# The first two steps of a fused attention and sparse feed-forward kernel rewritten as programs of their own

## The chip, the cores and the metric

The kernel runs on one core of one Trainium2 chip. The metric is the device time of one execution in microseconds (us), the median over the runs.

## The reference

Two branches read the same normalised rows; their sum is added to the input. Cut to what matters:

```python
xn = layernorm(x)                              # x: 4096 rows of 512
# attention branch
q, k, v = xn @ Wq, xn @ Wk, xn @ Wv            # 16 heads of 32; rotary on q and k
# chunks of 128 rows, with a state kv carried from chunk to chunk
out = (q * q_decay) @ kv + ((q @ k.T) * dmask) @ v
kv  = r_C * kv + (k * k_decay).T @ v
attn = rms_norm(out) @ Wo
# sparse feed-forward branch; W_syn 2048x512, W_out 512x2048
ternary(W) = clip(round(W / mean|W|), -1, 1) * mean|W|
z = xn @ ternary(W_syn).T + b_syn
hidden = where(z >= 204th largest of the row, relu(z), 0)
ffn = layernorm(xn + hidden @ ternary(W_out).T + b_out)
result = x + attn + ffn
```

## The kernel before

The 4096 rows are 32 tiles of 128. Every engine runs a program written out by hand: a prologue, then 34 calls of `step`. In step s four tiles are in work: `a` = s+2 (normalised and turned), `b` = s+1 (projections q, k, v and the four z pieces, numbers 0 to 6), `t` = s (attention, search for the threshold), `u` = s-1 (threshold applied, hidden rows split in a high and a low half and turned by DMA, `Wo`), and `d` = s-2 (`network`: the second feed-forward product, 32 matmuls `p_ffn`, and the output). Engines meet by counting semaphores; each engine and each DMA queue works strictly in the order of its program.

The prologue prepares the weights and the first tile up to its z. The mean of |W_syn| gives its threshold (`syn_thr`). ScalarE (ACT) takes row sums of |W|, TensorE adds them across partitions, and VectorE forms the threshold. Then VectorE (`ternary`) and ACT (`sign`, with `ternary_of_signs` on VectorE) make the ternary weights, which are turned by TensorE or by DMA transposes (`synT0`, `synT2`; `outT0` to `outT3`). The four quarters of W_out are prepared during steps 0 and 1, where memory is tight: they pass through places that later hold something else. Quarter 1 (`outT1`) sits in the low half of `hl`, so the first `lo_ready` (tile 0's low half, on GpSimd, which the page calls POOL) waits until that transpose has landed; VectorE's `below` for tile 1 writes `masked` and waits for this `lo_ready`. `hT`, which takes the turned hidden rows, lies over the buffer `area1[:, 3N:4N]`, through which quarters 0 and 1 of W_out are loaded (`out_in[0]`, loaded twice, and `out_in[1]`).

SP issues nearly all DMAs; ACT issues only the four loads of W_syn, among its first sums. `network(0)` starts when all four `outT` and the high half of tile 0 in `hT` are there, and needs the low half for its second 16 matmuls.

```python
wait(dve, "lo_ready", t, 1, 0)       # below(t): tile t-1's low half is made
if u.n == 0:
    pool.wait_ge(S["outT1"], 16)     # tile 0's low half
for q in range(4):
    pe.wait_ge(S[f"outT{q}"], 16)    # network, tile 0
```

## Time and profile before

| | us |
|---|---|
| median of 3 runs | 1045.2 (1045.08 to 1045.99) |
| the profiled execution: its time | 1045.96 |
| the profiled execution: its span | 1044.0 |
| busy TensorE (PE) | 971.1 (93%) |
| busy VectorE (DVE) | 760.7 (73%) |
| busy ScalarE (ACT) | 560.8 (54%) |
| busy GpSimd (POOL) | 694.9 (67%) |

The span is what the profiler covers; some 2 us lie around it. The shares are averages over stages: in 40 slices of the span TensorE is busy 1, 7, 6 and 7 tenths in the first four and 9 or more from the sixth to the 37th.

### The profile page before, as it was taken

What the parts mean: (1) busy time and instruction counts of PE and PEld (TensorE: products, weight loads), DVE (VectorE), ACT (ScalarE), POOL (GpSimd) and SP (SyncE); (2) the same over time, 40 slices, a digit from 0 to 9 for tenths busy, and PEclk for the clock granted to TensorE, in tenths of its full rate; (3) what the DMA queues carried; (4) which work ended last, traced back from release to release, by engine and by line L of the source; (5) the groups of instructions that cost most, each with busy time, mean ns of one, the idle gap of its engine ahead of it and who ended that gap; (6) DMA issues with size and microseconds to landing.
All of it is one profiled execution on the core that took longest, in us unless ns stands there. A gap on an engine that the chain in (4) does not pass through costs nothing.

```text
span 1044.0 us, 18566 instructions
## 1 busy us (share of the span) xinstructions
PE 971.1 (93%) x6608; PEld 493.5 (47%) x6608; DVE 760.7 (73%) x2153; ACT 560.8 (54%) x715; POOL 694.9 (67%) x617
## 2 busy tenths in 40 slices
PE   1767799999999999999999999999999999999875
PEld 0333455554555555554555555554555555554432
DVE  2577767777877777777877777777877777776762
ACT  3877664654454665654455655654455655654421
POOL 1334777777778777777778777777777777777522
PEclk9978899999999999999999999999999999999976
DMA  9785756546455456545654555455554455555322
GB/s 295 258 201 91 145 88 112 101 92 112 100 103 96 83 96 112 97 97 111 97 107 78 96 101 111 92 101 111 93 111 89 81 104 110 89 106 101 72 51 60
DMA packets 328782, 113.65 MB, mean 109 GB/s; under 512 B 314736, under 2 KB 314992, under 8 KB 327792
## 3 DMA queue, kind: packets, MB, share of 16 engines
q1 hardware_dynamic: 326576, 108.25, 53.5%
q10 hardware_dynamic: 2112, 4.19, 1.3%
q8 instruction: 53, 0.87, 0.3%
q14 instruction: 41, 0.34, 0.1%
HBM read 25.38 MB, written 8.39 MB: 32 GB/s over the span
## 4 chain that ended last, share of the span: by engine, by line
PE 84%; DVE 1%; DMA 1%; issue 0%; POOL 0%; ACT 0%; SPq 0%; POOLq 0%; DVEq 0%
PE proj L735 42%; PE p_ffn L828 22%; PE p_wo L864 10%; PE p_av L803 3%; PE sbank L794 3%; PE p_av L849 2%; PE sbank L743 1%; PE sbank L885 1%; DMA area<-hl 1%; DVE area L1136 0%; PE sbank L897 0%; ACT hl L475 0%; PE p_wo L814 0%; POOL c L636 0%; SPq L299 0%
## 5 line engine op out<-in xcount | busy, mean ns | idle before, releaser
L735 PE MATMUL proj<-wqkv,xT 128*128 128x512 f16 x1152 | 257.6, 383 | 0.7 <-DVE wqkv L967 0.4
L735 PE MATMUL proj<-wsynT,xT 128*128 128x512 f16 x1024 | 246.2, 384 | 1.4 <-DVE area L1022 0.9
L828 PE MATMUL p_ffn<-woutT,area 128*128 128x512 f16 x1024 | 235.6, 385 | 10.9 <-DMA area<-hl 10.9
L735 PEld LDWEIGHTS proj<-wqkv,xT 128*128 128x128 f16 x1152 | 113.2, 99 | 131.7 <-issue 4.0
L468 ACT ACTIVATE Pr<-area,c 128x2048 f16<-128x2048 f32 x32 | 64.1, 2003 | 199.0 <-DVE c L1130 193.4
L828 PEld LDWEIGHTS p_ffn<-woutT,area 128*128 128x128 f16 x1024 | 101.9, 104 | 121.6 <-DMA area<-hl 11.1
L735 PEld LDWEIGHTS proj<-wsynT,xT 128*128 128x128 f16 x1024 | 93.2, 99 | 126.1 <-issue 35.0
L1022 DVE SCALAR_TENSOR_TENSOR area<-proj,c,gb 128x512 f32<-128x512 f32 x128 | 95.3, 745 | 42.8 <-PE proj L735 40.0
L631 POOL TENSOR_TENSOR hl<-area,hl 128x2048 f16<-128x2048 f32 x30 | 122.4, 4079 | 4.3 <-ACT hl L475 4.3
L864 PE MATMUL p_wo<-wo,pair_a 128*128 128x512 f32 x256 | 118.7, 607 | 0.0
L550 POOL TENSOR_TENSOR xhl<-xn,xhl 128x512 f16<-128x512 f32 x32 | 78.3, 2448 | 53.9 <-ACT xhl L397 53.9
L515 ACT ACTIVATE pair_a<-p_av 128x512 f32<-128x512 f32 x32 | 19.1, 597 | 173.3 <-PE p_av L803 167.5
L1091 DVE MAX8 cand<-area 128x8 f32<-128x128 f32 x512 | 110.4, 278 | 0.0
L544 POOL TENSOR_TENSOR c<-c 128x1 f32<-128x1 f32 x32 | 17.6, 550 | 135.2 <-DVE c L1012 135.2
L1074 DVE SCALAR_TENSOR_TENSOR Pr<-sbank,c,dmask 128x512 f32<-128x512 f32 x128 | 89.9, 744 | 0.6 <-ACT Pr L489 0.6
L578 POOL TENSOR_TENSOR area<-area 128x512 f16<-128x512 f32 x64 | 72.6, 1155 | 11.4 <-ACT area L405 11.4
L1136 DVE SCALAR_TENSOR_TENSOR area<-area,c 128x2048 f32<-128x2048 f32 x32 | 79.4, 2481 | 0.0
L1186 DVE SCALAR_TENSOR_TENSOR area<-area,c 128x2048 f32<-128x2048 f32 x32 | 75.3, 2352 | 0.8 <-POOL hl L631 0.7
L475 ACT ACTIVATE hl<-area 128x2048 f16<-128x2048 f32 x32 | 61.2, 1912 | 26.1 <-DVE area L1136 26.1
L864 PEld LDWEIGHTS p_wo<-wo,pair_a 128*128 128x128 f32 x256 | 47.1, 194 | 47.2 <-issue 47.0
L483 ACT ACTIVATE Pr<-area,c 128x2048 f16<-128x2048 f32 x32 | 64.1, 2003 | 2.0 <-DVE c L1148 1.2
L489 ACT ACTIVATE Pr<-area,c 128x2048 f16<-128x2048 f32 x32 | 63.6, 1989 | 1.7 <-DVE c L1175 1.7
(176 smaller groups left out, 1459.2 us busy)
## 6 DMA issues: line engine op xcount, KB each, us to landing
xr<-in_L_attn_x_dram SPq DMA_DIRECT2D x32, 256.0 KB, 3.2
out_dram<-pair_b SPq DMA_DIRECT2D x32, 256.0 KB, 2.1
area<-in_L_ffn_W_out_dram SPq DMA_DIRECT2D x3, 1024.0 KB, 6.0
woutT<-in_L_ffn_W_syn_dram ACTq DMA_DIRECT2D x2, 1024.0 KB, 13.2
area<-in_L_ffn_W_syn_dram ACTq DMA_DIRECT2D x2, 1024.0 KB, 17.7
woutT<-in_L_ffn_W_out_dram SPq DMA_DIRECT2D x2, 1024.0 KB, 6.5
area<-in_L_attn_Wq_dram SPq DMA_DIRECT2D x1, 1024.0 KB, 6.6
area<-in_L_attn_Wk_dram SPq DMA_DIRECT2D x1, 1024.0 KB, 9.7
```

The lines of the kernel that those rows point to most:

```text
L468: nc.scalar.activation(unused, z[:, t.par, :], ACT.Sign, bias=nt0, accum_out=s1).then_inc(S["sum1"], 1)
L550: nc.gpsimd.tensor_tensor(xhl[:, 1, :], slot(xn, a), xhl[:, 0, :], ALU.subtract).then_inc(S["xl_ready"], 1)
L578: nc.gpsimd.tensor_tensor(qks[:, m, :, 2 - m, :], qk[:, b.par, m * E:(m + 1) * E].rearrange("p (h d) -> p h d", h=H), qks[:, m, :, 0, :], ...
L631: nc.gpsimd.tensor_tensor(hl[:, 1, :], masked, hl[:, 0, :], ALU.subtract).then_inc(S["lo_ready"], 1)
L735: last = nc.tensor.matmul(bank, xT[:, b.par, k, :], w, start=m == 0, stop=m == len(pairs) - 1)
L828: last = nc.tensor.matmul(p_ffn, hT[:, k, :], woutT[:, k % NB, :], start=k == 0, stop=k == 2 * NB - 1)
L864: last = nc.tensor.matmul(p_wo, aT[:, g, :], wo[:, g, :], start=g == 0, stop=g == HG - 1)
L1022: nc.vector.scalar_tensor_tensor(z[:, b.par, n * 512:(n + 1) * 512], proj[(b.par + 3 + n) % 2], gs, gb[:, n * 512:(n + 1) * 512], ALU.mult ...
L1074: nc.vector.scalar_tensor_tensor(Pr[:, g % 2].rearrange("p j c -> p (j c)"), sbank[SCORES[g]], ppp, dmask[:, 4 * g:4 * g + 4, :].rearrange ...
L1091: nc.vector.max(cand[:, 0, 8 * n:8 * n + 8], masked[:, n * SEG:(n + 1) * SEG]).then_inc(S["seg_done"], 1)
L1136: nc.vector.scalar_tensor_tensor(masked, z[:, u.par, :], thr, z[:, u.par, :], ALU.is_ge, ALU.mult).then_inc(S["h_ready"], 1)
L1186: nc.vector.scalar_tensor_tensor(masked, z[:, t.par, :], t2, z[:, t.par, :], ALU.is_le, ALU.mult).then_inc(S["w_out"], 1)
```

## The change

It touches the prologue and steps 0 and 1 alone; from step 2 on the instructions and their order are the same on each engine.

1. Loads: ACT issues Wq, Wk, Wv and the four quarters of W_syn as its very first work; SP issues x of tiles 0 and 1, `ident`, then the small loads. `gb`, `gam` and the W_out quarter 0 follow the last quarter of W_syn.
2. Tile 1's halves stand apart: they use `xhl_second`, in `hl`, and each parity has its own semaphore `xT_ready`, so that tile 1 needn't wait for tile 0's transpose.
3. VectorE takes the |W_syn| sums of quarters 2 and 3 (`reduce_sum`), ACT keeps 0 and 1.
4. The threshold's sum (`sums_spread`) stands before tile 1's third projection, with `row_flipped(3)` and `row_spread(3)`.
5. GpSimd scales `wo` by `rms_w` in place of VectorE. ACT's counts for tile 0 write their unused output to `signs_a` and not to `Pr`, so VectorE's `probs` of tile 0 don't wait for them.
6. All four sums of |W_out| stand in ACT's prologue and their threshold in step 0; out quarter 3 is made ternary in step 0, quarters 2, 1 and 0 in step 1. Other scratch: `out_t[2]` is `free_x` (xr slots 3 and 4), `out_t[0]` is the first half of `area1[:, 3N:4N]`.
7. In step 1 TensorE's `failures` of tile 0 stands behind the first of tile 2's projections, not ahead of them.

```diff
-        out_t = [signs_a, hl[:, 1, :], hl[:, 0, :], free_xn]
+        out_other = [signs_b, hl[:, 0, :], signs_b, masked.bitcast(F16)[:, 0:N]]
+        xhl_second = hl[:, 0, 0:2 * E].rearrange("p (a n) -> p a n", a=2)
+        out_t = [area1[:, 3 * N:4 * N].bitcast(F16)[:, 0:N], hl[:, 1, :], free_x, free_xn]
...
             def prologue():
-                load_x(0)
+                first, second = tile(0), tile(1)
+                x_loaded(first)
+                x_loaded(second)
                 load(ident, t_ident, "ident_loaded")
-                for m, W in enumerate((Wq, Wk, Wv)):
-                    load(qkv_in[:, m], W.rearrange("(b p) n -> p b n", p=P), f"qkv_loaded{m}")
...
                 syn_transposed(0, 1)
                 load(out_in[2], wt[:, 2, :], "out_loaded2")
-                syn_transposed(2, 2)
-
                 sp.wait_ge(S["syn_sign"], 2)
                 load(out_in[3], wt[:, 3, :], "out_loaded3")
-                qk_transposed(Tile(0, 0))
-                sp.wait_ge(S["synT2"], 16)
-                load_x(3)
+                syn_transposed(2, 2)
...
+            def second_step():
+
+                out_transposed(2, 2)
+                out_transposed(3, 2)
+                sp.wait_ge(S["out_sign"], 4)
+                load(out_in[0], wt[:, 0, :], "out_loaded0")
+                sp.wait_ge(S["outT2"], 16)
+                x_loaded(tile(3))
+                x_loaded(tile(4))
+                out_transposed(1, 3)
+                x_transposed(tile(3))
+                out_transposed(0, 4)
+
+                sp.wait_ge(S["outT0"], 16)
+                hidden_high(tile(0))
+                hidden_low(tile(0))
+                qk_transposed(tile(2))
...
+            def load_first():
+                for m, W in enumerate((Wq, Wk, Wv)):
+                    act.dma_start(qkv_in[:, m], W.rearrange("(b p) n -> p b n", p=P)).then_inc(S[f"qkv_loaded{m}"], 16)
+                for q in range(4):
+                    act.dma_start(syn_in[q].rearrange("p (b d) -> p b d", d=E),
+                                  W_syn.rearrange("(b p) d -> p b d", p=P)[:, 4 * q:4 * q + 4, :]
+                                  ).then_inc(S[f"syn_loaded{q}"], 16)
...
             def prologue():
-                first, second = Tile(0, 0), Tile(0, 1)
+                first, second = tile(0), tile(1)
+                load_first()
                 normalised(first)
-                qkv_sums(0)
-                load_syn(0)
-                load_syn(1)
-                qkv_sums(1)
-                load_syn(2)
-                load_syn(3)
                 normalised(second)
-                qkv_sums(2)
+                for m in range(3):
...
+                for q in range(2, 4):
+                    dve.wait_ge(S[f"syn_loaded{q}"], 16)
+                    nc.vector.reduce_sum(pc[:, q:q + 1], syn_in[q], AX.X,
+                                         apply_absolute_value=True).then_inc(S["syn_absv"], 1)
```

Three places of the order of instructions.

ACT, the first rows of its program, of the kernel before (its DMA rows are the loads of W_syn):

```order
L394 ACT_TABLE_LOAD
L394 ACTIVATE xn<-xr,c 128x512
L397 ACTIVATE xhl<-xr,c 128x512
L366 ACTIVATE pair_b,pc<-area 128x2048
L375 DMA woutT<-in_L_ffn_W_syn_dram 128x4x512 x2
L366 ACTIVATE pair_b,pc<-area 128x2048
L375 DMA area<-in_L_ffn_W_syn_dram 128x4x512 x2
```

The same place of the changed kernel:

```order
L357 DMA area<-in_L_attn_Wq_dram 128x4x512
L357 DMA area<-in_L_attn_Wk_dram 128x4x512
L357 DMA area<-in_L_attn_Wv_dram 128x4x512
L359 DMA woutT<-in_L_ffn_W_syn_dram 128x4x512 x2
L359 DMA area<-in_L_ffn_W_syn_dram 128x4x512 x2
L407 ACT_TABLE_LOAD
L407 ACTIVATE xn<-xr,c 128x512
L411 ACTIVATE xhl<-xr,c 128x512
```

Seven loads of 1 MB now stand ahead of ACT's first computation.

SP, from the transposes of W_out to those of tile 0's hidden rows (`woutT` rows are outT2, outT3, outT1 and outT0; `area<-hl` the high and the low half of the hidden rows), of the kernel before:

```order
L299 DMA_TRANSPOSE woutT<-hl 128x16x128
L299 DMA_TRANSPOSE woutT<-xn 128x16x128
L299 DMA_TRANSPOSE woutT<-hl 128x16x128
L225 DMA area<-in_L_ffn_W_out_dram 128x2048
L251 DMA_TRANSPOSE xT<-xhl 128x8x128
L299 DMA_TRANSPOSE woutT<-pair_a 128x16x128
L308 DMA_TRANSPOSE area<-hl 128x16x128
L319 DMA_TRANSPOSE area<-hl 128x16x128
```

The same place of the changed kernel:

```order
L276 DMA_TRANSPOSE woutT<-xr 128x16x128
L276 DMA_TRANSPOSE woutT<-xn 128x16x128
L223 DMA area<-in_L_ffn_W_out_dram 128x2048
L223 DMA xr<-in_L_attn_x_dram 128x512 x2
L276 DMA_TRANSPOSE woutT<-hl 128x16x128
L245 DMA_TRANSPOSE xT<-xhl 128x8x128
L276 DMA_TRANSPOSE woutT<-area 128x16x128
L254 DMA_TRANSPOSE area<-hl 128x16x128
L258 DMA_TRANSPOSE area<-hl 128x16x128
```

The load of W_out and two loads of x have moved ahead of outT1, and a wait for outT0's landing stands ahead of the hidden rows.

VectorE, step 1 behind tile 0's threshold (`area<-area` is tile 0's hidden rows; `L928` and `L1037` are `ternary_of_signs`, `L1028` and `L1142` `q_decayed` of tile 1), of the kernel before:

```order
L928 TENSOR_TENSOR hl<-hl,pair_b 128x2048
L1136 SCALAR_TENSOR_TENSOR area<-area,c 128x2048
L1028 SCALAR_TENSOR_TENSOR pair_c<-sbank,c,qdec 128x512
L1008 BN_STATS st<-xr 128x6
L1010 BN_AGGR c<-st 128x2
```

The same place of the changed kernel:

```order
L1209 SCALAR_TENSOR_TENSOR area<-area,c 128x2048
L1142 SCALAR_TENSOR_TENSOR pair_c<-sbank,c,qdec 128x512
L1037 TENSOR_TENSOR xr<-xr,pair_b 128x2048
L1037 TENSOR_TENSOR hl<-hl 128x2048
L1215 TENSOR_SCALAR c<-c 128x1
```

Quarters 2 and 1 of W_out are made ternary behind tile 0's hidden rows and behind `q_decayed` of tile 1, and the row statistics of tile 3 have moved from here to a place behind `below` and the first two `probs`.

## Rows read from the trace of the kernel before

**Rows 1.** Busy time by stage: start:end, length, engines, clock, DMA share, GB/s.

```profile
0.00:44.00 44.00, 20.08 (x82) 8.88 (x83) 15.18 (x37) 24.44 (x26) 13.12 (x21) 1.00 0.98 321
...
92.00:128.00 36.00, 27.39 (x173) 14.01 (x174) 26.25 (x60) 26.62 (x26) 19.55 (x16) 0.86 0.68 124
128.00:158.00 30.00, 30.00 (x208) 15.24 (x207) 21.66 (x63) 15.96 (x21) 21.38 (x19) 1.00 0.54 99
```

**Rows 2.** Chain that ended last, around the first `network`: start, length, what.

```profile
118.38 1.27 DVE pair_a L928
...
119.67 1.86 SPq L299
...
121.57 6.26 DMA area<-hl
...
127.87 3.63 PE p_ffn L828 x16
```

**Rows 3.** Timelines of the first 46 us: start, length, engine, line, what.

```profile
8.32 1.91 ACT L366 ACTIVATE pair_b<-area 128x2048 f16<-128x2048 f32 x1 [1.21 <-DMA area<-in_L_attn_Wq_dram]
...
17.79 0.69 DVE L1008 BATCH_NORM_STATS2 st<-xr 128x6 f32<-128x512 f32 x1 [12.24 <-DMA xr<-in_L_attn_x_dram]
...
45.65 1.29 DVE L921 TENSOR_SCALAR pair_a<-woutT,pc 128x2048 f16<-128x2048 f32 x1
...
24.03 3.59 PE L735 MATMUL proj<-wqkv,xT 128*128 128x512 f16 x8 [0.30 <-DMA xT<-xhl]
```

**Rows 4.** ACT's issues of the W_syn loads, from the timeline.

```profile
8.33 1.04 ACTq L375 DMA_DIRECT2D woutT<-in_L_ffn_W_syn_dram  x2
...
12.25 2.17 ACTq L375 DMA_DIRECT2D area<-in_L_ffn_W_syn_dram  x1
```

**Rows 5.** SP's issues, from the timeline.

```profile
53.45 4.34 SPq L263 DMA_TRANSPOSE wsynT<-xr  x1
...
97.26 1.93 SPq L299 DMA_TRANSPOSE woutT<-hl  x1
99.24 3.53 SPq L299 DMA_TRANSPOSE woutT<-xn  x1
103.19 1.32 SPq L299 DMA_TRANSPOSE woutT<-hl  x1
104.55 1.31 SPq L225 DMA_DIRECT2D area<-in_L_ffn_W_out_dram  x1
```

**Rows 6.** DMA issues at 53, 104, 119 and 137: size, us to landing.

```profile
wsynT<-xr SPq DMA_TRANSPOSE x1, 7.2
...
area<-in_L_ffn_W_out_dram SPq DMA_DIRECT2D x1, 1024.0 KB, 6.0
...
woutT<-pair_a SPq DMA_TRANSPOSE x1, 4.4
...
area<-hl SPq DMA_TRANSPOSE x1, 4.3
```

**Rows 7.** VectorE's timeline, steps 0 and 1.

```profile
67.69 0.43 DVE L1057 SCALAR_TENSOR_TENSOR c<-pc 128x1 f32<-128x1 f32 x1
...
91.20 0.16 DVE L1246 TENSOR_TENSOR c<-c 128x1 f32<-128x1 f32 x1
...
106.00 0.69 DVE L1008 BATCH_NORM_STATS2 st<-xr 128x6 f32<-128x512 f32 x1
...
111.91 2.35 DVE L1186 SCALAR_TENSOR_TENSOR area<-area,c 128x2048 f32<-128x2048 f32 x1 [0.73 <-POOL hl L631]
...
125.84 0.13 DVE L1227 TENSOR_SCALAR c<-c 128x1 f32<-128x1 f32 x1
```

**Rows 8.** Timelines of TensorE (q, k, v of tiles 2 and 3) and of POOL.

```profile
92.35 9.62 PE L735 MATMUL proj<-wqkv,xT 128*128 128x512 f16 x36
...
135.36 7.93 PE L735 MATMUL proj<-wqkv,xT 128*128 128x512 f16 x36
...
107.74 4.07 POOL L631 TENSOR_TENSOR hl<-area,hl 128x2048 f16<-128x2048 f32 x1
```

More of the change, by code:

```diff
@@ L200, in apart, with x_turned, tile @@
             eng.sem_inc(S["passed"], 1)
+        def x_turned(eng, a):
+            eng.wait_ge(S[f"xT_ready{a.par}"], a.half * 16 + 16)
         def slot(ring, t):
             return ring[:, t.n % RING, :]
-        def run_steps(eng, step):
-            for s in range(NT + 2):
-                step(eng, s // 2, s % 2)
-        def stage(i, p, k):
-            t = Tile(i, p + k)
-            return t if 0 <= t.n < NT else None
+        def tile(n):
+            return Tile(n) if 0 <= n < NT else None
         @block.sync
@@ L659, in _ @@
             prologue()
-            run_steps(pool, step)
+            first_step()
+            second_step()
+            for s in range(2, NT + 2):
+                step(s)
         @block.tensor
@@ new lines, in first_step @@
+            def first_step():
+                first, second = tile(0), tile(1)
+                inter(first)
+                for g in range(3):
+                    scores(first, g)
+                projection(second, 3)
+                sums_spread("out")
+                scores(first, 3)
+                values(first, 0)
+                values(first, 1)
+                projection(second, 4)
+                values(first, 2)
+                values(first, 3)
+                projection(second, 5)
+                keys_values(first)
+                projection(second, 6)
+                square_sum(first)
@@ L857, in step @@
                 if u:
[L859 to L865 removed]
+                    attention_projected(u)
                 if b:
@@ new lines, in first_step @@
+            def first_step():
+                first, second, third = tile(0), tile(1), tile(2)
+                dve.wait_ge(S["dmask_loaded"], 16)
+                probs(first, 0)
+                probs(first, 1)
+                row_stats(third)
+                mean_abs("out", 18, scale_out, out_thr)
+                then(nc.vector.scalar_tensor_tensor(so, scale_out, 0.5 * XS / 16384.0, pc[:, 43:44], ALU.mult, ALU.mult))
+                first_count(first)
+                row_shift(third)
+                z_chunk(second, 0)
+                probs(first, 2)
+                probs(first, 3)
+                second_count(first)
+                dve.wait_ge(S["syn_flip"], 8)
+                ternary("out", out_in[3], out_t[3], out_other[3], out_thr)
+                dve.wait_ge(S["out_tern"], 1)
+                below(first)
+                z_chunk(second, 1)
+                segments(first, 0)
+                segments(first, 1)
+                z_chunk(second, 2)
+                segments(first, 2)
+                segments(first, 3)
+                z_chunk(second, 3)
+                top_values(first)
@@ new lines, in second_step @@
+            def second_step():
+                first, second, third, fourth = tile(0), tile(1), tile(2), tile(3)
+                state_updated(first)
+                threshold(first)
+                hidden(first)
+                q_decayed(second)
+                ternary_of_signs("out", out_t[2], out_other[2], 2)
+                ternary_of_signs("out", out_t[1], out_other[1], 4)
+                first_count(second)
+                second_count(second)
+                below(second)
+                probs(second, 0)
+                probs(second, 1)
+                row_stats(fourth)
+                segments(second, 0)
+                row_shift(fourth)
+                z_chunk(third, 0)
+                probs(second, 2)
+                probs(second, 3)
+                segments(second, 1)
+                z_chunk(third, 1)
+                attention_added(first)
+                segments(second, 2)
+                z_chunk(third, 2)
+                segments(second, 3)
+                ternary_of_signs("out", out_t[0], out_other[0], 6)
+                top_values(second)
+                z_chunk(third, 3)
@@ L1139, in step @@
+            def step(s):
+                a, b, t, u, d = tile(s + 2), tile(s + 1), tile(s), tile(s - 1), tile(s - 2)
+                if u:
+                    state_updated(u)
+                    threshold(u)
+                    hidden(u)
+                if t:
                     q_decayed(t)
```

869 lines of the change are left out of this document (463 added, 406 removed).

## The prediction

> **What bounds the kernel now.** I read the busy time by stage first. From 128 us on TensorE is busy 30.00 of 30 us at full clock, while VectorE has 21.7 and DMA half; before that it has 20.1 of 44 us and 27.4 of 36 [rows 1]. The change leaves everything from step 2 on as it is, so it can only move the moment at which step 2 starts, that is `network(0)` at 127.87 us. No cover stands behind that moment: what it moves, the end moves. The chain of waits says what makes that moment: `ternary_of_signs` of W_out's last quarter at 118.38 on VectorE, its transpose issued at 119.67, the hidden-row transpose behind it, and the matmuls at 127.87 [rows 2]. So the question is when that chain ends in the new order. I follow it in four stretches, each against a time mark of the old trace.
>
> **Stretch 1, to the threshold of W_syn (old: 45.65 [rows 3]).** Before, x of tile 1 came at 17.79, behind 3 MB of weights in SP's queue, and VectorE waited 12.24 us for it, with tile 0's first scale factors queued behind; TensorE's first projection began at 24.03, when tile 0's turned rows had landed [rows 3]. With x first, this wait goes. What is late next is ACT, which now issues seven 1 MB loads ahead of its first computation. The trace prices such issues: the first two W_syn loads took 1.04 together, but the fourth one in ACT's queue took 2.17, though nothing but a full queue stood in its way [rows 4]; on SP a transpose behind one unfinished 1 MB load took 4.34 to issue [rows 5]. ACT's queue thus holds somewhat over 3 MB (the fourth load went in when about 1 MB had gone), and each further load waits until another MB has gone. At the stage's 321 GB/s [rows 1] the seventh goes in when its queue has moved 3.9 MB and SP's 0.6 MB of x and `ident`: 4.7e6 bytes / 321 = 14.7 us; with a slower start I take 16 (bounds: 4, if the queue never fills, and 17). Then come the table load, two pairs of normalisations (estimated 5 us together, from the change's eight short ACT and VectorE steps) and the first |W| sum of 1.9 [rows 3], which was over at 10.2 and now is at about 23; before, VectorE got to it some 2 us behind x, at about 20. So TensorE's first projection starts some 2.7 us later, at 26.7.
>
> A rule of the Trainium skill (DMA: Bandwidth & Descriptors, "Issuing engines are not separate DMA queues") says that starting DMAs on several engines only saves the sequencer's time, usually small beside the DMA. The 321 GB/s that one stretch of both queues made agrees in so far as no bandwidth is to be had. Taken alone, with every issue as short as the shortest rows, it gives ACT back at about 4 us, and the result of the third case below.
>
> The threshold now needs five of six projections ahead of it and not six. Three take 7.93 us at full clock [rows 8], so one is worth 2.6. Together: +2.7 - 2.6 and some tenths for the moved transpose and factors: threshold at 45, 0.6 earlier. VectorE's two sums over 128x2048 are in no row; between a 2048-wide pass of 1.29 [rows 3] and one of 2.35 [rows 7] each, I take 2.3, being reductions. 4.6 us lie beside TensorE's projections (VectorE idles there), cost nothing, and would cost up to 2 if TensorE were 2 us faster. ACT loses two sums and so keeps up.
>
> **Stretch 2, to the first guess (old: 67.69 [rows 7]).** The last z pieces of tile 0 wait for W_syn quarter 2's transpose, which landed at 53.45 + 7.2 = 60.65 with one load of W_out ahead of it [rows 5, 6]. Now two loads stand ahead. 1 MB at 321 GB/s is 3.3 us; issued 1 to 2 us earlier, and below the worst case, I take +1.5 (bounds 0 and 3.3). The guess comes at 69.5, +1.8 with the rest.
>
> **Stretch 3, to tile 0's failure flag (old: 91.20 [rows 7]).** It took 23.5. VectorE gains that `probs` no longer wait for ACT's third count, and loses the W_out threshold and the three passes of a ternary quarter (4.6). Counted piece by piece (4 `probs`, statistics, counts, ternary, `below`, 4 z, 16 maxima, top) it is 21.8. Flag at 91.3: no change. GpSimd's four `wo` products are in no row; between 1 and 4 us each (the latter is its 2048-wide pass [rows 8]), they lie in its idle time ahead of the guess.
>
> **Stretch 4, from the flag to `network(0)` (old: 36.6).** Here the new order makes one long chain.
> 1. VectorE does tile 0's threshold and hidden rows early (done at 96, which no one needs yet), then stands at `q_decayed` of tile 1 until TensorE has done two of tile 2's projections and the transposes: 24 matmuls, 5.3 at full clock and 6.4 at the old one [rows 8], from 91.8, then 1.3 for transposes and `q_decayed`: 98.7. Queued behind it are both `ternary_of_signs`: 100.0 for quarter 2. Before, its transpose was issued at 97.26 [rows 5].
> 2. SP issues outT2 (1.93) and outT3 (3.53), as before [rows 5], but then W_out's load (1.31 [rows 5]) and two x loads, and only then outT1. Before, outT1 went at 103.19 and landed 4.4 later, 10.4 after outT2's issue. Now 1.5 MB is ahead of it in the same queue: 1.57e6 / 321 = 4.9, at the best rates 4.1. Landed at 100.0 + 10.4 + 4.1 = 114.5.
> 3. POOL's `hidden_low` waits for that, as before (107.74, 4.07 [rows 8]): to 118.6. VectorE's `below` of tile 1 waits for `hidden_low`: the old row says so too, 111.91 with 0.73 of idle left to POOL [rows 7]. Now 118.7.
> 4. From `below` to the first top step took 13.9 [rows 7], with 3.2 of waiting for and doing the last quarter, and now has tile 3's statistics in it, 1.3 (the first of them is 0.69 [rows 7]): 12.1. `ternary_of_signs` of quarter 0 follows at 130.8, ready 132.1 (ACT's signs, at 129, are not late).
> 5. outT0 is issued and lands 4.4 later [rows 6]: 136.5. Its source lies in `hT`, so SP waits for the landing, and only then turns the hidden rows: 4.3 [rows 6]: 140.9. Before, both were in the queue together, 8.2 from 119.67 to 127.87 [rows 2].
>
> `network(0)` starts at 141.0, +13.1. TensorE has idled for some 6 us by then. In the old trace 36 matmuls took 9.62 after such a gap and 7.93 in the full stream [rows 8]: +1.7. Behind it TensorE is full and nothing is given back. Everything else that step 2 needs (x of tiles 3 and 4, q and k of tile 2) is there before.
>
> **The sum.** Stretch 1 -0.6, stretch 2 +2.4, stretch 3 -1.7, stretch 4 +13.0, clock +1.7: +14.8 on the span of 1044.0, so 1058.8, and 1060.8 with the 1.96 around it. The median of before stands 0.8 under its profiled run: 1060.0.
>
> **The rivals.** *Forecast: the queue fills and the chain of stretch 4 holds.* 1060, its own range 1055 to 1066. Chance 0.60.
> *Third case: ACT's issues never block* (the rule's way). For: SP's own first loads show no stall. Against: the 2.17. The threshold then comes 11 us earlier, but DMA stays busy to 44 us [rows 1] and behind it stand the turned q and k, synT0, two loads and synT2, four transposes at some 2 us and two loads at 2.8, so quarter 2 lands at about 57.7 and not 62.2: -4.5, and 1055.5. Chance 0.20.
> *The head start is kept.* Before, tile 0's hidden rows waited for quarter 1's signs; now they are ready 9.5 us earlier (96 for 105.4, just ahead of the statistics at 106.00 [rows 7]). If `network(0)` followed them, 127.87 - 9.5 = 118.4, and the result 1035.7. It decides if outT1 lands before about 100, so that `below` and the last quarter aren't held. Against it: outT1 stands behind three loads, which the order shows. Chance 0.10.
> *A half-kept chain*: the loads overtaken or tile 1's quarters earlier, so that stretch 4 gains back most: 1043 to 1052. Chance 0.10, of which 0.04 lies within 0.2% of before.
>
> **How the numbers follow.** This kernel's runs let one tell 0.2% (2.1 us) from no change. Slower: 0.60 + 0.20 + 0.05 = 0.85; same 0.04; faster 0.11. The range leaves out the kept head start and the ends: from 1049 (blocked queue empty, late loads cheap) to 1066 (second load's full 3.3, slow clock in tile 2's projections, 1.3, and in the z pieces of step 1).
>
> **What would show it.** Right: ACT's last W_syn load issued near 14 to 16 us and its first activation behind it; the threshold near 45; outT1 landing 13 or more after outT2's issue; `below` of tile 1 released by POOL at about 118; outT0's landing ended SP's wait at about 136; `network(0)` at about 141, and from there the same distance to the end (916 us). Wrong: ACT's first activation at 5 us; VectorE's tile 1 `below` at 112 or before; `network(0)` under 128.

## The result and the profile after

The changed kernel takes 1066.76 us (median of 4 runs, 1065.95 to 1067.77) against 1045.6 of the kernel before in the same session: ratio 1.0203, 95% interval 1.0185 to 1.0221. It is slower by 21.2 us, on the side that was forecast, 0.8 beyond the upper end of the range and 6.8 above the number. The profiled execution took 1066.48, its span is 1064.7 (before: 1044.0).

Busy time by stage of the kernel after; columns as in [rows 1].

```profile
0.00:46.00 46.00, 21.16 (x78) 9.39 (x79) 22.00 (x44) 23.83 (x25) 12.58 (x21) 1.00 0.92 311
46.00:72.00 26.00, 19.16 (x132) 12.25 (x131) 21.34 (x23) 19.32 (x21) 16.17 (x10) 0.80 0.83 196
...
98.00:147.00 49.00, 22.95 (x160) 11.16 (x159) 25.67 (x63) 23.52 (x25) 20.08 (x19) 0.79 0.58 114
147.00:177.00 30.00, 30.00 (x198) 14.75 (x197) 17.98 (x44) 15.95 (x21) 17.00 (x14) 0.94 0.49 86
```

From 147 us on TensorE has no gap, as it had none from 128 on before. In the 49 us ahead of that no engine is busy for much over half of the time: a chain of waits. It ends where the old one did, at `network(0)`. The rows of the chain of work that ended last (start, length, what):

```profile
57.33 7.61 DMA wsynT<-xr
65.08 5.31 PE proj L815 x16
...
106.88 3.58 SPq L276
112.09 7.58 DMA woutT<-hl
119.81 4.06 POOL hl L646
...
137.47 4.26 DMA woutT<-area
141.75 4.47 DMA area<-hl
146.27 5.84 PE p_ffn L912 x16
```

`network(0)` starts at 146.27 (127.87 in [rows 2]), 18.4 later, and its first 16 matmuls take 5.84 (3.63 there), 2.2 more: 20.6 of the span's 20.7. So the whole loss lies ahead of step 2, and nothing behind it adds or gives back. The timelines show where it arose. ACT's queue and ACT, first 14 us:

```profile
0.73 0.46 ACTq L357 DMA_DIRECT2D area<-in_L_attn_Wq_dram  x1
...
2.33 4.74 ACTq L359 DMA_DIRECT2D woutT<-in_L_ffn_W_syn_dram  x2
7.10 5.30 ACTq L359 DMA_DIRECT2D area<-in_L_ffn_W_syn_dram  x2
12.43 1.28 ACT L407 ACT_TABLE_LOAD   x1 [12.43 <-issue]
13.73 0.81 ACT L407 ACTIVATE xn<-xr,c 128x512 f32<-128x512 f32 x1
```

Three loads go in at half a microsecond each; the last four hold ACT for 10 us. VectorE's first three of six passes for W_syn, which start at the threshold, then the first guess (73.67), the failure flag (97.33), and `q_decayed` and `below` of tile 1:

```profile
44.93 2.41 DVE L1030 TENSOR_SCALAR pair_a<-woutT,pc 128x2048 f16<-128x2048 f32 x1
47.38 2.18 DVE L1031 TENSOR_SCALAR hl<-woutT,pc 128x2048 f16<-128x2048 f32 x1
49.59 2.17 DVE L1032 TENSOR_TENSOR hl<-pair_a,hl 128x2048 f16<-128x2048 f16 x1
...
73.67 0.16 DVE L1319 SCALAR_TENSOR_TENSOR c<-pc 128x1 f32<-128x1 f32 x1
...
97.33 0.16 DVE L1266 TENSOR_TENSOR c<-c 128x1 f32<-128x1 f32 x1
...
103.60 0.75 DVE L1142 SCALAR_TENSOR_TENSOR pair_c<-sbank,c,qdec 128x512 f32<-128x512 f32 x1 [1.41 <-PE sbank L823]
...
123.97 2.35 DVE L1234 SCALAR_TENSOR_TENSOR area<-area,c 128x2048 f32<-128x2048 f32 x1 [12.22 <-POOL hl L646]
```

And GpSimd at the same moments (L613 is `qk_low` of tile 0, L590 and L591 are the additions of the biases):

```profile
42.76 2.27 POOL L613 TENSOR_TENSOR area<-area 128x512 f16<-128x512 f32 x2 [1.96 <-ACT area L419]
44.99 1.26 POOL L590 TENSOR_TENSOR xn<-xn,boutx 128x512 f32<-128x512 f32 x1
46.22 2.25 POOL L591 TENSOR_TENSOR xr<-xr,bet 128x512 f32<-128x512 f32 x1
48.43 2.25 POOL L590 TENSOR_TENSOR xn<-xn,boutx 128x512 f32<-128x512 f32 x1
```

The first and the last of the same four additions in the kernel before:

```profile
40.49 1.26 POOL L555 TENSOR_TENSOR xn<-xn,boutx 128x512 f32<-128x512 f32 x1
...
44.16 1.26 POOL L556 TENSOR_TENSOR xr<-xr,bet 128x512 f32<-128x512 f32 x1
```

The pass that took 1.29 in [rows 3] takes 2.2 to 2.4 here (four of the six; the last two take 1.95 and 1.30), and GpSimd's additions go from 1.26 to 2.25: the two take turns. Their place is new. Before, GpSimd had done these four additions ahead of the threshold, which stood at 45.65. The changed kernel puts `qk_low` of tile 0 ahead of them in GpSimd's program, where it stood behind them before; the list of the change does not name this move. So they start only at 44.99, with the passes.

By the four stretches of the prediction and its clock term (to the threshold, to the guess, to the flag, to `network(0)`, clock): -0.7, +6.7, +0.1, +12.3, +2.2.

### The profile page after: what moved, and what is told of

It is laid out like the page before. It is cut to its first block, busy times and chain, and to the rows that moved or that the text cites. A ratio compares the mean times of both kernels' runs of the same rounds, so it can differ in the third digit from the quotient of the medians.

```text
span 1064.7 us, 18560 instructions
## 1 busy us (share of the span) xinstructions
PE 973.2 (91%) x6608; PEld 492.9 (46%) x6608; DVE 773.6 (73%) x2151; ACT 556.3 (52%) x707; POOL 705.3 (66%) x621
## 4 chain that ended last, share of the span: by engine, by line
PE 86%; DVE 6%; DMA 3%; ACTq 1%; POOL 1%; issue 1%; ACT 1%; SPq 0%; POOLq 0%; DVEq 0%
PE proj L815 43%; PE p_ffn L912 21%; PE p_wo L897 10%; PE p_av L860 3%; PE sbank L851 2%; PE p_av L833 2%; PE sbank L823 1%; PE sbank L871 1%; ACTq L359 1%; DMA area<-hl 1%; DMA xT<-xhl 1%; DMA wsynT<-xr 1%; DMA woutT<-hl 1%; DVE Pr L1153 1%; DVE cand L1242 1%
## 5 line engine op out<-in xcount | busy, mean ns | idle before, releaser
L912 PE MATMUL p_ffn<-woutT,area 128*128 128x512 f16 x1024 | 238.0, 388 | 14.5 <-DMA area<-hl 14.5
L578 POOL TENSOR_TENSOR c<-c 128x1 f32<-128x1 f32 x96 | 56.6, 590 | 221.0 <-DVE c L1126 130.5
L442 ACT ACTIVATE Pr<-area,c 128x2048 f16<-128x2048 f32 x31 | 62.1, 2002 | 198.5 <-DVE c L1204 198.5
L585 POOL TENSOR_TENSOR xhl<-xn,xhl 128x512 f16<-128x512 f32 x31 | 74.0, 2386 | 59.0 <-ACT xhl L411 59.0
L1234 DVE SCALAR_TENSOR_TENSOR area<-area,c 128x2048 f32<-128x2048 f32 x32 | 76.1, 2379 | 12.3 <-POOL hl L646 12.2
L613 POOL TENSOR_TENSOR area<-area 128x512 f16<-128x512 f32 x64 | 72.6, 1155 | 2.0 <-ACT area L419 2.0
L419 ACT ACTIVATE area<-area 128x1024 f16<-128x1024 f32 x64 | 64.1, 1057 | 12.9 <-POOL area L608 12.9
L450 ACT ACTIVATE Pr<-area,c 128x2048 f16<-128x2048 f32 x31 | 61.7, 1989 | 2.2 <-DVE c L1228 2.2
## 6 DMA issues: line engine op xcount, KB each, us to landing
woutT<-in_L_ffn_W_syn_dram ACTq DMA_DIRECT2D x2, 1024.0 KB, 14.5
area<-in_L_ffn_W_syn_dram ACTq DMA_DIRECT2D x2, 1024.0 KB, 14.5
```

The lines of the kernel that those rows point to most:

```text
L419: nc.scalar.activation(qks[:, m, :, 0:2 + m:1 + m, :], src.unsqueeze(2).to_broadcast([P, H, 2, DH]), ACT.Copy).then_inc(S["qk_hi"], 1)
L585: nc.gpsimd.tensor_tensor(xs[:, 1, :], slot(xn, a), xs[:, 0, :], ALU.subtract).then_inc(S["xl_ready"], 1)
L613: nc.gpsimd.tensor_tensor(qks[:, m, :, 2 - m, :], qk[:, b.par, m * E:(m + 1) * E].rearrange("p (h d) -> p h d", h=H), qks[:, m, :, 0, :], ...
L912: last = nc.tensor.matmul(p_ffn, hT[:, k, :], woutT[:, k % NB, :], start=k == 0, stop=k == 2 * NB - 1)
L1234: nc.vector.scalar_tensor_tensor(masked, z[:, t.par, :], t2, z[:, t.par, :], ALU.is_le, ALU.mult).then_inc(S["w_out"], 1)
```

## The experiments

Theory A, formed from the two traces: the loss is two chains in series, the forecast one of stretch 4 (outT1 behind three loads, then `hidden_low`, `below`, the last quarter, outT0) and one that was not forecast: VectorE and GpSimd block each other in stretch 2 (and 3), which moves the whole chain later. Rivals: the seven loads on ACT are the cause; the second W_out load ahead of synT2 is; or the product of `wo` moved to GpSimd is. Each kernel is the kernel after with the edit shown, if nothing else is said. Its distance is taken from 1066.8. The changed kernel was measured in its first session alone, and the kernel before stood at 1045.2 to 1046.4 from session to session, so such a distance is good to about 1 us. The ratios are to the kernel before in the same session.

**Additions held behind the passes.**

```
                 qk_low(first)
-                pool.wait_ge(S["bout_ready"], 1)
+                pool.wait_ge(S["syn_tern"], 2)
                 biases(first)
```

GpSimd's decayed v and its `wo` products stand behind the additions in its program and are held with them.

> GpSimd's bias additions, decayed v and wo products wait until VectorE has made both quarters of W_syn ternary. Theory A (VectorE and GpSimd slow each other down in the ternary passes): the passes of 2.2 to 2.4 us fall back to about 1.3, the second quarter is ready near 53 instead of 57.3 us, its transpose lands near 62 instead of 65, and the time falls by 2.5 to 4 us against the changed kernel (1066.8), to 1063 to 1064. Rival B (the passes are slow for another reason, or only the order of the two W_out loads holds the transpose): passes stay above 2 us or the landing stays at 65, no change.

1060.78 us, ratio 1.0134 (1.0117 to 1.0151): 6.0 gained. VectorE's and TensorE's timelines:

```profile
43.24 1.29 DVE L1030 TENSOR_SCALAR pair_a<-woutT,pc 128x2048 f16<-128x2048 f32 x1
44.56 1.28 DVE L1031 TENSOR_SCALAR hl<-woutT,pc 128x2048 f16<-128x2048 f32 x1
45.88 1.23 DVE L1032 TENSOR_TENSOR hl<-pair_a,hl 128x2048 f16<-128x2048 f16 x1
...
60.53 3.61 PE L815 MATMUL proj<-wsynT,xT 128*128 128x512 f16 x16 [1.76 <-DMA wsynT<-xr]
```

The six passes take 7.8 us again and not 12.4. From threshold to guess it is 24.2 us and not 28.7, so 4.5 are gained there: synT2 lands 17.2 us behind the threshold and not 20.0, and TensorE, which waits 1.76 for it and not 2.98, takes 3.61 for the 16 matmuls behind the wait and not 5.30, at the granted clock of 1.00 (0.71 from 66 to 71 us in the kernel after). The transpose itself takes 9.1 from issue to landing (7.6 in the kernel after), since it is issued 6 us earlier, close behind the two loads.

The threshold also falls at 43.24 and not 44.93, and that is no effect of the edit. Kernels alike up to that point show 43.0 to 43.4 in five profiles and 44.6 to 44.9 in three. The traces show where the two kinds part: from 30 to 32 us TensorE starts 6 or 7 matmuls of the projections in the three late profiles and 10 or 11 in the five early ones, so it goes at half the pace for some us, though the granted clock of the profile reads 1.00 in all eight. What decides between the two stays open. Single runs of one kernel spread by 2 to 6 us as well, so a difference of one profile under 2 us is not read as an effect below.

**outT1 ahead of the loads.**

```
                 out_transposed(3, 2)
+                out_transposed(1, 3)
                 sp.wait_ge(S["out_sign"], 4)
...
                 x_loaded(tile(4))
-                out_transposed(1, 3)
```

> In step 1 the transpose outT1 goes ahead of the load of W_out and the two loads of x. Theory A (the chain outT1, hidden_low on GpSimd, below on VectorE, last quarter, outT0, hidden rows, network(0)): outT1 lands 4 to 5 us earlier, at about 115 instead of 119.7, and the time falls by as much, to about 1062. Rival B (another wait, tile 3's rows or the signs of quarter 0 that need the load, ends last): less than 1 us.

1061.25 us, 1.0141 (1.0124 to 1.0158): 5.5 gained. GpSimd's `hidden_low` starts at 115.41 (119.81), `below` of tile 1 waits 8.03 for it (12.22), `network(0)` is at 142.03 (146.27). The passes are still 2.1 to 2.2 here. Of these 4.2 to 4.4 us, 1.4 are there at the flag already, by the earlier threshold of this profile; from outT2's issue to the start of `hidden_low` it is 9.5 us and not 14.3. So the link of stretch 4 that the prediction named is real and about as large as the 4.1 that it had for the loads; `below` is still 7.7 later than in [rows 7].

**W_syn's loads behind the normalisations.**

```
                 normalised(second)
+                load_syn(0)
+                load_syn(1)
                 for m in range(3):
                     qkv_sums(m)
+                    if m < 2:
+                        load_syn(2 + m)
```

> ACT issues Wq, Wk, Wv first as now, but the four loads of W_syn only behind both normalisations and among its first sums. Theory A (a full queue holds ACT until 12.4 us): the first activation starts at about 4 to 5 us instead of 12.4, the threshold of W_syn comes 5 to 8 us earlier, and after DMA's limits 3 to 5 us of it remain in the time, 1062 to 1064. Rival B (the loads set all): the threshold moves, the first guess does not, no change. Rival C: the issues just block ACT later, ahead of its sums: under 2 us.

1063.05 us, 1.0158 (1.0141 to 1.0175): 3.7 gained. ACT computes at 6.10 and not 13.73, TensorE's first projection is at 18.07 and not 25.27, and the threshold at 36.2. But SP's queue gives nearly all of that back:

```profile
34.88 11.00 SPq L265 DMA_TRANSPOSE area<-area  x2
...
47.95 1.50 SPq L223 DMA_DIRECT2D woutT<-in_L_ffn_W_out_dram  x2
49.50 7.29 SPq L270 DMA_TRANSPOSE wsynT<-xr  x1
```

The turned q and k take 11 us to issue (4.57 in the kernel after), and synT2 is issued behind two loads and lands 9.4 us later (7.6). Of 8.8 us at the threshold 3.7 reach the end in the median (5.8 in the profiled run, the fastest of the four): that ACT is held costs time, but the transfers behind it set most of it. The first four of the six passes take 2.1 to 2.2 here, too.

**`wo` back on VectorE** (its four products in the wait for W_syn's pieces, none on GpSimd).

```
-                pool.wait_ge(S["wo_loaded"], 2 * 16)
-                for k in range(KB):
-                    nc.gpsimd.tensor_tensor(wo[:, k, :], ...)
...
                         q_decayed(first)
+                    if n == 1:
+                        dve.wait_ge(S["wo_loaded"], 2 * 16)
+                        for k in range(KB):
+                            nc.vector.tensor_scalar(wo[:, k, :], ...)
```

> The four wo products go back to VectorE, into its wait for the last pieces of tile 0's z; GpSimd's other work stays. If these products are what slows VectorE: ternary passes back at 1.3 and 3 us or more gained. If it is the bias additions that now stand beside the ternary passes: passes stay at 2.2, only the scaling of gb (2.03) and the step beside it get shorter, and the time changes by less than 1 us.

1067.21 us, 1.0188 (1.0169 to 1.0207): nothing gained that is clear of noise. The passes stay as they were (2.42, three of 2.17 to 2.18, 1.95, 1.30). So the products are not the cause; that the additions are, the run in the kernel before shows, below.

**synT2 ahead of the second W_out load.**

```
+                syn_transposed(2, 2)
                 sp.wait_ge(S["syn_sign"], 2)
                 load(out_in[3], wt[:, 3, :], "out_loaded3")
-                syn_transposed(2, 2)
```

> The changed kernel with the transpose of W_syn's quarter 2 issued ahead of the load of W_out's quarter 3. Theory A (the second load holds the transpose up, as the prediction's stretch 2 had it): it lands 1.5 to 3.3 us after its issue less than before, 4.5 to 6 instead of 7.6 us, and 1.5 to 3 us of time are gained. Rival B (that quarter is formed only at 57.3 us, when most of the load has gone): under 1 us.

1061.62 us, 1.0153 (1.0135 to 1.0170): 5.1 gained, where 1.5 to 3 were expected. SP's queue and TensorE:

```profile
55.10 2.98 SPq L270 DMA_TRANSPOSE wsynT<-xr  x1
...
60.03 1.89 PE L815 MATMUL proj<-wsynT,xT 128*128 128x512 f16 x8 [1.48 <-DMA wsynT<-xr]
```

The transpose lands some 5 us earlier than in the kernel after (TensorE goes on at 60.03 and not 65.08), though it is issued only 2.2 earlier, 1.9 of which are the earlier threshold of this profile. It takes 4.8 from issue to landing and not 7.6, and TensorE, with 1.5 us of idling and not 3.0, keeps its full clock, which is worth 1.7 on 16 matmuls. From threshold to guess it is 24.5 and not 28.7. This is as much as holding the additions gave, with the passes still at their 2.1 to 2.2: each of the two repairs alone takes 4.3 to 4.5 of the 6.7 that stretch 2 lost.

**The slow-down put into the kernel before**: there the additions are held until W_syn's threshold stands.

```
                 pool.wait_ge(S["bout_ready"], 1)
+                pool.wait_ge(S["syn_thr"], 1)
                 biases(first)
```

> The kernel before with one edit: GpSimd's bias additions wait for W_syn's threshold, so that they stand beside VectorE's ternary passes, as in the changed kernel. Theory A (the two engines slow each other down): passes of 1.29 become 2.1 to 2.4, additions of 1.26 become 2.2, W_syn's quarter 2 is ready 3 to 4 us later and the time rises by 3 to 5 us, 1.003 to 1.005 of before. Rival B (the additions are harmless, something else in the changed kernel slows the passes): passes stay at 1.3 and the time within 1 us.

1047.94 us, 1.0021 (1.0010 to 1.0033): slower by 2.2, where 3 to 5 were expected. The passes lengthen to 2.17 as in the kernel after (the first three):

```profile
44.34 1.29 DVE L922 TENSOR_SCALAR pair_a<-woutT,pc 128x2048 f16<-128x2048 f32 x1
45.67 2.17 DVE L923 TENSOR_SCALAR hl<-woutT,pc 128x2048 f16<-128x2048 f32 x1
47.88 2.17 DVE L924 TENSOR_TENSOR hl<-pair_a,hl 128x2048 f16<-128x2048 f16 x1
```

All four additions of GpSimd take 2.24 to 2.31 here, one of them:

```profile
46.72 2.25 POOL L556 TENSOR_TENSOR xr<-xr,bet 128x512 f32<-128x512 f32 x1
```

So the long passes are reproduced where nothing else was changed. What they cost is less sure. The ten runs fall in two groups, four at 1045.3 to 1045.7, as the kernel before, and six at 1047.9 to 1050.3, and the profiled run is the fastest of the first group. In its trace the threshold is 1.3 us earlier than in [rows 3], as TensorE's first projection is 1.4 earlier, ahead of anything that the edit touches. Counted from the threshold, the six passes take 11.4 and not 7.8, the guess comes 1.8 later, the flag 1.2 and `network(0)` 1.05. So of 3.6 us under a third reaches the end in this trace: synT2 is issued 3.65 behind the load ahead of it and not 1.9, and lands 5.1 behind its issue and not 7.2. The 1.05 lies within the interval of the ratio (1.0 to 3.4 us).

**W_out's quarters in another order.** outT3, outT2 and outT1 ahead of tile 1's turned q and k, their signs and sums in step 0, the last quarter summed as soon as tile 0's attention is added.

```
 # SP, step 0
                 x_transposed(tile(2))
+                sp.wait_ge(S["out_sign"], 2)
+                out_transposed(3, 1)
+                out_transposed(2, 2)
+                out_transposed(1, 3)
                 qk_transposed(tile(1))
...
 # VectorE, step 0
                 z_chunk(second, 3)
+                ternary_of_signs("out", out_t[2], out_other[2], 2)
+                ternary_of_signs("out", out_t[1], out_other[1], 4)
                 top_values(first)
```

> Only the order of the four W_out quarters in steps 0 and 1 is changed: ACT makes the signs of quarters 2 and 1 ahead of its high halves of q and k of tile 1, VectorE forms both quarters ahead of tile 0's top values, SP transposes quarters 3, 2 and 1 at once and ahead of the load of W_out and of x. Theory A (from tile 0's flag on, outT1 and what waits for it sets network(0)): outT1 lands near 102 instead of 119.7, below of tile 1 starts near 113 instead of 124 and network(0) near 135 instead of 146: 1055 or 10 to 13 us less than the changed kernel. Rival B (step 1 is held by something else that comes as late, such as tile 1's own threshold search or tile 3's rows): under 5 us less.

1055.99 us, 1.0100 (1.0084 to 1.0117): 10.8 gained, as expected. The profiled run took 1051.35 and the other three 1055.8 to 1056.4, so the rows are those of a run that is over 4 us faster than the median; its `network(0)` is at 131.70, where 135 was expected. The whole wait of stretch 4 for outT1 is gone; `below` of tile 1 now waits 1.78 for `hidden_low`:

```profile
95.12 1.97 SPq L276 DMA_TRANSPOSE woutT<-hl  x1
...
110.69 2.35 DVE L1235 SCALAR_TENSOR_TENSOR area<-area,c 128x2048 f32<-128x2048 f32 x1 [1.78 <-POOL hl L647]
...
121.66 1.22 DVE L1038 TENSOR_TENSOR area<-area,pair_b 128x2048 f16<-128x2048 f16 x1 [1.31 <-ACT area L378]
```

**That order and the held additions.**

> The kernel with W_out's quarters reordered in steps 0 and 1 (1056.0), plus the bias additions held behind W_syn's ternary passes, which alone gave 6.0. If the two are separate terms of one chain, they add: 1066.8 - 10.8 - 6.0 = 1050.0. If the chain of step 1 in the reordered kernel hangs on transfers and not on VectorE, the second gives less than half: 1053 to 1056.

1050.83 us, 1.0046 (1.0033 to 1.0059): 15.9 of the 16.8 that the two gave alone, so the two chains add, as theory A has it, within the spread: three of the ten runs took 1046.7 to 1047.0 (granted clock 0.977 over the whole run), the other seven 1050.0 to 1052.6 (0.971 to 0.974).

**Held additions in step 0 as well.** To the hold of the first experiment comes:

```
                 low_half(tile(2))
-                biases(tile(2))
+                pool.wait_ge(S["w_out"], 1)
                 rotary(tile(1))
                 squares(tile(0))
                 qk_low(tile(1))
+                biases(tile(2))
```

> The kernel after, with GpSimd's work held off VectorE's 2048-wide passes in both places: the bias additions behind the ternary passes of W_syn, and in step 0 the rotary step behind `below` of tile 0, with the additions of tile 2 last. If the two engines slow each other, the passes of the third W_out quarter (1.28, 2.07, 2.17 in the kernel after) and `below` (3.23) fall to about 1.28, 1.23, 1.29 and 2.35, the failure flag comes 6 us behind its place in the kernel after through the first hold and 2 to 2.6 us more through the second, and all of it reaches `network(0)`: 1066.8 - 6.0 - 2.3 = 1058.5. Rival: the passes of step 0 are long for their layout or element type, GpSimd's later rotary step only delays the turned q and k, and the time stays at the 1060.8 of the first hold alone or goes 1 to 2 us above it.

1061.71 us, 1.0151 (1.0137 to 1.0166), against 1060.8 with the first hold alone: nothing gained, and the number expected was missed by 3.2. The trace shows why. The third pass (1.22 and not 2.17) and `below` (2.35 and not 3.23) did become short, 1.8 us together, and two small steps at the end of the top values became long, by 1.9 together:

```profile
79.89 1.22 DVE L1033 TENSOR_TENSOR xn<-area,xn 128x2048 f16<-128x2048 f16 x1
81.15 2.35 DVE L1235 SCALAR_TENSOR_TENSOR area<-area,c 128x2048 f32<-128x2048 f32 x1
...
91.21 1.17 DVE L1260 SCALAR_TENSOR_TENSOR sel<-iota,c,top 128x32 f32<-128x32 f32 x1
...
92.49 1.09 DVE L1265 TENSOR_TENSOR c<-c 128x1 f32<-128x1 f32 x1
```

GpSimd's two additions lie at 91.07 and 92.29, 1.26 and 1.27 long:

```profile
92.29 1.27 POOL L591 TENSOR_TENSOR xr<-xr,bet 128x512 f32<-128x512 f32 x1
```

The second of VectorE's steps, over one element per partition, takes 0.15 elsewhere and 1.09 here; it ends at 93.58, the addition at 93.56, and the first ends at 92.38 beside an addition that ends at 92.33. From guess to flag it is 23.8 us (23.7 in the kernel after): the cost was moved and not removed. A place in which VectorE waits for something else should remove it; the last experiment tries that.

**All repairs**: the reordered quarters, the first hold, the split loads, synT2 ahead of the second load.

> The order of the run before, with GpSimd's biases held until W_syn is ternary (e1), with ACT's W_syn loads behind its normalisations (e3), and with the transpose of W_syn's quarter 2 ahead of the second W_out load. Theory A (the losses are separate links of one chain and add up): some 6 for the quiet ternary passes, 4 for the loads, 10 to 13 for the order, 1 to 3 for the transpose: 1066.8 - 22 to 26, that is 1041 to 1045, at or under the kernel before. Rival B (the DMA traffic of the first 44 us caps the first two gains, which overlap): 1047 to 1052.

1046.80 us (10 runs, 1044.0 to 1050.3), 1.0009 (0.9994 to 1.0023): level with the kernel before, and short of the 1041 to 1045 that theory A gave. `network(0)` starts at 128.30. Alone the four repairs gave 6.0, 10.8, 3.7 and 5.1, together 25.6; here they give 20.0. Three of them work on the same wait, that for synT2: each of these alone brings the guess to 67.5 to 67.7, and all together to 65.1.

**Four more moves in steps 0 and 1**: the hold of step 0; W_out's quarter 1 summed behind the state update; tile 1's first count and tile 0's hidden high half ahead of what waits for TensorE; the last quarter ahead of tile 3's rows. The core of the diff against all repairs:

```
 # VectorE, step 1
                 state_updated(first)
+                ternary_of_signs("out", out_t[1], out_other[1], 4)
                 threshold(first)
                 hidden(first)
-                q_decayed(second)
                 first_count(second)
+                q_decayed(second)
 # ACT, step 1
                 heads_state(second)
-                qkv_out(third, 1)
                 first_count(second)
+                qkv_out(third, 1)
+                hidden_high(tile(0))
+                second_count(second)
                 qkv_out(third, 2)
...
```

> The kernel of all repairs (1046.8) with four more moves in steps 0 and 1: GpSimd's rotary step of tile 1 behind `below` of tile 0 (2.6 us of VectorE), the second W_out quarter summed behind the state update and not ahead of tile 0's flag (1.2 to 2.2), tile 1's first count and tile 0's hidden high half ahead of the work that waits for TensorE (3 to 4 for `below` of tile 1), and the last W_out quarter ahead of tile 3's normalisation and turned rows, with its transposes first in SP's queue. The flag should come at 86 to 88 (92.0 in the kernel of all repairs), `below` of tile 1 at 101 to 103 (107.3), the last quarter's transpose be issued at 107 to 111 (119.5), and `network(0)` start at 116 to 121 (128.3; before: 127.87), as TensorE's own work ahead of it ends at about 113. The time then is 1046.8 - 8 to 12 = 1035 to 1039, below the kernel before. Rival: the DMA traffic of the last W_out load, two x loads and the turned q and k delays the quarter's signs past 112, and the time stays between 1040 and 1046.

1040.56 us, 0.9957 (0.9943 to 0.9972): faster than the kernel before by 0.4%, but behind the expected 1035 to 1039 and inside the rival's 1040 to 1046. It got there in another way than the rival's: the last quarter's sum, at 111.79, follows VectorE's own work and does not wait for ACT's signs. `below` of tile 1 is at 104.31 and `network(0)` at 122.86, 1.3 and 1.9 us behind the latest that was expected: the flag came only at 91.7 (86 to 88 expected). The additions of tile 2 stood beside its last steps again (0.86 at 89.60, 1.07 at 90.57), which is 1.5 of it; in this profile the guess, too, is 1.8 later than in that of all repairs (66.91 for 65.10), and I found no part of the edit that explains that.

**Those additions in VectorE's gap**, and the last quarter summed right behind tile 3's statistics:

```
                 decayed(tile(1))
+                pool.wait_ge(S["h_ready"], 1)
+                biases(tile(2))
                 hidden_low(tile(0))
```

> The best kernel so far (1040.6) with GpSimd's two additions of tile 2 moved into the gap in which VectorE waits for TensorE (behind tile 0's hidden rows, ahead of the hidden low half), and the last W_out quarter summed right behind tile 3's statistics. If each of GpSimd's operations costs VectorE about 0.9 us wherever it meets one of its 2-byte passes or its tensor-tensor steps, and nothing where VectorE idles, then the two long last steps of tile 0's top values (0.86 and 1.07) fall to 0.25 and 0.15, the flag comes 1.5 to 1.9 us earlier (90.6 to 91.9 there), and q and k, `below` of tile 1 and the rest with it. The last quarter's transpose is issued near 109 (113.86), and `network(0)` starts at 118 to 120 (122.86), as TensorE's own work of step 1 ends near 116: 1036 to 1038. Rival: the cost is not in the overlap (the last steps of the top values are long for another reason, or `hidden_low` is late because the additions stand ahead of it): `below` of tile 1 keeps its place or comes later, and only the earlier transpose counts, with at most 2 us: 1039 to 1042.

1038.38 us (6 runs, 1035.65 to 1039.80), 0.9926 (0.9911 to 0.9942), 0.4 above the expected 1036 to 1038. The last steps of the top values are short. The flag is at 88.25, 3.4 earlier, of which 1.9 are there at the guess already and 1.5 come behind it, as expected. GpSimd's additions run at their own 1.27, while VectorE does three short steps, each at its own length, and then waits 2.63 for ACT:

```profile
87.70 0.25 DVE L1267 SCALAR_TENSOR_TENSOR sel<-iota,c,top 128x32 f32<-128x32 f32 x1
...
88.07 0.15 DVE L1272 TENSOR_TENSOR c<-c 128x1 f32<-128x1 f32 x1
...
94.24 1.27 POOL L596 TENSOR_TENSOR xn<-xn,boutx 128x512 f32<-128x512 f32 x1 [2.58 <-DVE area L1217]
...
119.36 0.58 PE L888 MATMUL sbank<-ones,pair_a 128*128 128x1 f32 x2 [3.45 <-POOL pair_a L659]
119.80 6.46 PE L920 MATMUL p_ffn<-woutT,area 128*128 128x512 f16 x16
```

`network(0)` now starts 8.1 us ahead of its old place, without a wait of its own: what ends last ahead of it is GpSimd's sum of squares, for which TensorE idles 3.45. 2.8 of the gain are lost behind that gap, at a granted clock of 0.55 (6.46 for the 16 matmuls, 3.63 in [rows 2]). This version is 7.3 us faster than the kernel before and 28 faster than the changed one. It keeps parts of the change: Wq, Wk and Wv in ACT's queue, x first, tile 1's halves apart. So these can stand in a faster kernel, and most of the loss lay in the order of loads, transposes and additions around them.

## Why the prediction was right in direction and too low in size

**Bound and point of decision: right.** It said that only the start of step 2 can move and that what it moves, the end moves: 20.6 at the first matmuls of step 2, 20.7 at the end.

**Stretch 1: right, in part by luck.** -0.7 against -0.6, with the threshold at 44.93 for 45. ACT's last load was in at 12.40 and not 16, and the first projection at 25.27 and not 26.7; from there to the threshold it took 19.7 and not 18.3. Two errors cancel, and the second is the half pace of the matmuls at 30 us, which only three of eight profiles show; the other five put the threshold at 43.0 to 43.4. The row of 2.17 for a fourth load [rows 4] was enough to see that the queue fills: the fifth to seventh load took over 2 us each. VectorE's two sums took 4.47 (4.6 taken) and cost nothing. The rule that several issuing engines only save the sequencer's time (the Trainium skill, DMA: Bandwidth & Descriptors, "Issuing engines are not separate DMA queues") holds for bandwidth, as 311 GB/s over the first 46 us against 321 shows; the third case that was built on it fell, since the issuing engine was itself held for 10 us.

**Stretch 2: the step that failed.** It had +2.4 and measured +6.7. The prediction kept the passes at the 1.29 of [rows 3] and asked of GpSimd's work only whether GpSimd had time for it, not whom it runs beside. The passes took 12.4 us for six and not 7.8, so synT2 was issued 4.6 later behind the threshold; it landed 20.0 us behind the threshold and not 15.0; and behind the gap of 3 us that this left, the slow clock cost TensorE 1.7, for which the sum had nothing. 5.0 and 1.7 are the 6.7. The run with the additions held shows the same from the other side: with the passes at 1.29 the guess comes 24.2 behind the threshold, +2.2 on the kernel before, where the forecast had +2.4; and synT2 takes 9.1 from issue to landing and not the 7.2 of [rows 6], +1.9 for the second load, where it had +1.5. So the term for the load was right, and what was left out was the meeting of the two engines, and the clock behind it. Moving `wo` back gave nothing, and the same additions in the kernel before made its passes as long and cost it 2.2 (1.0 to 3.4). That this held kernel takes 1060.8, close to the forecast of 1060.0, is in part luck: its threshold is 2.4 earlier than before for a forecast of 0.6, and stretch 3 gives back nothing of the forecast 1.7.

The long passes are not the only way to see this wait: with them left long, synT2 ahead of the second load gave as much. In the changed kernel the loss needs both the late issue and the load in front of it.

The Trainium skill states a mechanism (SBUF — State Buffer, "Who interferes with whom"): VectorE and GpSimd share a port pair as an exclusive lock, and a VectorE instruction in a two-port mode, or one with two SBUF inputs beside a GpSimd instruction that reads SBUF, waits for the whole of the other's instruction. The trace agrees: 1.29 becomes 2.17, 1.26 becomes 2.25, and z pieces read from PSUM (0.73 to 0.75) and the maxima with one input (1.63 for 8) keep their time beside GpSimd. No run here separates this port from another cause that would make the same instructions take turns. I had weighed no rule of that page, and it was the one that spoke against this change.

**Stretch 3: a size.** 23.7 and not 21.8. The third quarter's passes and `below` met GpSimd's low half, additions and rotary step (2.07, 2.17 and 3.23 where 1.28, 1.22 and 2.35 are their own): 2.6, of which the count had nothing. That its gain of 1.7 did not come is the same error as in stretch 2, though taking two of the three meetings away gained nothing, as the cost moved to the top values. The four `wo` products, 1.5 each, ended at 62.17, well ahead of the guess, as the prediction had it.

**Stretch 4: right.** +12.3 against +13.0. Each link stands in the trace, all of them some 5 us later than the forecast had them: `ternary_of_signs` behind `q_decayed` (1.41 of waiting for TensorE), outT1 landed 14.2 after outT2's issue at 105.51 (forecast 14.5), `hidden_low` behind it, `below` 12.22 late through it, outT0 landed at 141.7 and the hidden rows turned only then. outT1's own landing took 7.58 beside the loads.

**Clock.** +2.2 against +1.7 at `network(0)`.

**The rivals.** ACT's first activation at 13.73 rules out the third case; `network(0)` at 146 and `below` at 124 rule out the kept head start and the half-kept chain. The range's upper end had the second load's full 3.3 and two slow clocks in it, but no term for engines that hold each other: stretches 2 and 3 are 6.1 above their forecasts together, and the whole span is 5.9 above its own.

**Open.** Why TensorE goes at half the pace at 30 us in three of eight profiles of kernels that are alike up to there; and why the kernel before with the delayed additions has two groups of runs, some 2.5 us apart, of which only the faster one was profiled.

## What to carry to other kernels

When a change moves work to another engine or to another moment, ask of each moved operation what it will run beside: where VectorE's and GpSimd's instructions took turns here, a pass of 1.29 and an addition of 1.26 together took 2.2 us, most of their sum. Here the cost went away where the operation stood at a place in which the other engine waits; moved off one instruction, it fell on the next. And in a queue, a transpose that a chain waits for goes ahead of every load that nobody waits for yet.

## What the runs showed of the hardware

A VectorE step over 128x1 that takes 0.15 took 1.07 to 1.09 beside a GpSimd addition of 1.26, and 0.35 to 0.39 where it met only the end of one: in each of these rows the step ends within 0.05 us of GpSimd's instruction. ACT's queue took three 1 MB loads at 0.5 us each, and the next two pairs held the engine for 4.74 and 5.30 us. 16 matmuls of 512 columns took 3.61 at the granted clock of 1.00, behind 1.02, 1.76 and 2.02 us of idling at the same place, and 5.30 behind 2.98, 3.18 and 3.23 us of it (0.71 over the 5 us from 66 in the kernel after).
